# Dense feed-forward of a two-layer network: gate and up products on moments of a row instead of on the whole row

## The reference, cut to what matters

```python
# layer 0, dense feed-forward; h is the layer-normed x, 2048 rows (4 batches x 512) of 512
gate_w, up_w = spline_reconstruct(gate_cp, 2048, 512), spline_reconstruct(up_cp, 2048, 512)
down_w = spline_reconstruct(down_cp, 512, 2048)
inter = silu(einsum('bsh,ih->bsi', h, gate_w)) * einsum('bsh,ih->bsi', h, up_w)
x = x + einsum('bsi,hi->bsh', inter, down_w)
# layer 1, the scan that the same stage computes beside it (16 states n, 512 channels d, 512 steps, 4 batches)
state = state * exp(dt * A) + (dt * u) * b
y = sum over n of state * c
```

## Time and profile before

| | |
|---|---|
| runs | 1562.31, 1568.68, 1570.82 us |
| profiled execution, first to last instruction | 1567.3 us |
| busy: PE, DVE, ACT, POOL | 1435.0, 1153.4, 918.4, 1062.3 us |
| block B | 180 to 818 us |

### The profile page before, as it was taken

The page is one execution under the profiler, slowest core; times in us unless marked ns, Lnnn a source line. Parts: engine busy times, 40 slices in busy tenths (PEclk is TensorE's granted clock), DMA queues, the critical chain, the costliest instruction groups (busy, mean ns, idle before and its releaser), DMA issues. The chain is left out here.

```text
span 1567.3 us, 26498 instructions
## 1 busy us (share of the span) xinstructions
PE 1435.0 (92%) x6453; PEld 1073.9 (69%) x6454; DVE 1153.4 (74%) x2069; ACT 918.4 (59%) x1420; POOL 1062.3 (68%) x654
## 2 busy tenths in 40 slices
PE   6999878999999999999975559989999999999997
PEld 3444556666666666666644238878988888898886
DVE  5888897888888878888878786656666666565554
ACT  6777677666667666766646664444544444444442
POOL 2222287999999989999941235757666676666675
PEclk9999989999999999999988759999999999999999
DMA  8232557888899889988869416889998899888876
GB/s 314 96 111 98 180 132 144 179 197 205 192 196 217 186 195 178 221 188 195 176 150 336 159 31 159 193 193 209 198 200 192 191 206 201 203 186 190 189 146 118
DMA packets 106416, 283.95 MB, mean 181 GB/s; under 512 B 16641, under 2 KB 18850, under 8 KB 95090
## 3 DMA queue, kind: packets, MB, share of 16 engines
q0 software_dynamic: 43520, 155.57, 50.0%
q1 hardware_dynamic: 60322, 123.12, 26.4%
q10 hardware_dynamic: 2512, 4.52, 0.8%
HBM read 152.28 MB, written 135.08 MB: 183 GB/s over the span
## 5 line engine op out<-in xcount | busy, mean ns | idle before, releaser
L1156 POOL TENSOR_TENSOR B_E<-B_dtu,B_BC 128x512 f32<-128x512 f32 (+3 forms) x121 | 309.3, 2670 | 16.7 <-DMA B_BC<-bc_d 16.7
L2080 POOL DMA_INDIRECT out_x<-D_y,D_rows x144 | 243.8, 1693 | 75.4 <-issue 43.6
L889 ACT ACTIVATE bank<-B_dtv,negA 128x512 f32<-128x512 f32 x256 | 173.5, 690 | 159.8 <-DVE B_E L1024 98.1
L1024 DVE TENSOR_TENSOR_SCAN B_E<-bank,B_E 128x512 f32<-128x512 f32 x192 | 230.2, 1214 | 42.5 <-ACT bank L889 34.8
L1162 POOL TENSOR_TENSOR B_E<-B_E,B_BC 128x1536 f32<-128x1536 f32 x64 | 234.0, 3656 | 34.5 <-DVE B_E L1024 29.8
L2045 POOL DMA_INDIRECT D_rows<-rows_d,D_source x144 | 155.9, 1083 | 129.0 <-DMA out_x<-D_y,D_rows 62.3
L806 PE MATMUL bank<-B_Wd,B_inter 128*128 128x512 f32 x512 | 231.9, 606 | 9.0 <-DVE X L1011 5.3
L1906 ACT ACTIVATE D_xT_hi<-bank 128x512 fp32r<-128x512 f32 x147 | 88.1, 599 | 231.5 <-PE bank L1815 167.8
L1826 PE MATMUL bank<-W_gu_hi,D_xT_hi 128*128 x584 | 202.4, 347 | 14.5 <-ACT D_xT_hi L1906 13.9
L1968 DVE TENSOR_TENSOR D_xT_lo<-bank,D_xT_hi 128x512 fp32r<-128x512 f32 x147 | 101.3, 689 | 141.1 <-ACT D_xT_hi L1906 108.7
L1827 PE MATMUL bank<-W_gu_lo,D_xT_hi 128*128 x584 | 199.2, 341 | 0.0
(11 more groups left out here) (327 smaller groups left out, 3263.7 us busy)
## 6 DMA issues: line engine op xcount, KB each, us to landing
y_d<-B_E POOLq DMA_DIRECT2D x64, 1024.0 KB, 10.7
B_BC<-bc_d SPq DMA_DIRECT2D x128, 256.0 KB, 6.2
W_raw_gu<-in_wgu SPq DMA_DIRECT2D x64, 384.0 KB
W_raw_d<-in_wd SPq DMA_DIRECT2D x64, 256.0 KB
X<-in_x SPq DMA_DIRECT2D x4, 1024.0 KB, 9.2
y_d<-A_du SPq DMA_DIRECT2D x4, 1024.0 KB, 4.0
dt_d<-A_dtv SPq DMA_DIRECT2D x4, 1024.0 KB, 3.9
dtu_d<-A_dtu SPq DMA_DIRECT2D x4, 1024.0 KB, 4.1
```

Source lines behind the costliest of these rows:

```text
L889: act.activation(dA[m % 2][:, :], dtv[:, c, :], ACT.Exp, scale=negA[:, c, n:n + 1]).then_inc(dA_done, 1)
L1024: v.tensor_tensor_scan(state, dA[m % 2][:, :], E[:, s % NR, c, :], 0.0, ALU.mult, ALU.add).then_inc(s_done, 1)
L1156: g.tensor_tensor(E[:, s % NR, c:end, :], dtu[:, at:at + end - c, :], spread(BC[op % NBC][:, :], end - c), ALU.mult).then_inc(dbu_done, 1)
L2080: g.indirect_dma_start(a["out"], bass.IndirectOffsetOnAxis(ap=rows[i][:, ROW - 1:ROW].bitcast(U32), axis=0), ysb[:, i, :], None, compute_o ...
```

## The change

- The features. For each of eight groups of 256 inner rows (`NG`), rows are sorted so that those of a group have the change of knot at about the same place. For every turn PE first makes F: four matmuls of 32 columns each, side by side in the array by `tile_position`, one for each chunk of 128 hidden values, in plain fp32. 32 features stand for a chunk: four moments each of two runs, and up to 24 values taken plainly. F is split into high and low parts (ACT L936, DVE L1040), and gate and up are products of 128 features: 12 matmuls a turn (L840 to L842) where there were 48.
- The order of turns. All weights are kept on chip (`V_hi`, `V_lo`, `Wd`). The outer loop is over batches, the inner one over the eight groups. Turned X is made for one batch at a time, in the last turn of the batch before.
- The down product sums four chunks in PSUM before it is added to X: `sums_at(jj)` gives two tiles a turn of 4 matmuls each. The number of matmuls is the same, the additions are two a turn instead of four, and both go through one bank (`Y_bank`, bank 5) because bank 4 holds F. The products of a turn are used one to three turns later (`NI` is 8), and the last four tiles come behind the last turn.
- 24 weight units, not 48: one for gate and up of a group and sixteen for down. All lie in turns 0 to 6, one to five a turn. Masks and powers are loaded three units ahead by ACT (L907, L908), 64 KB each.
- ACT makes both silus of a turn one behind the other, so it changes the table twice a turn instead of four times; F's high part stands behind them, ahead of the decays of the second step.
- Block A: the spline coefficients are plain fp32, without three low parts a batch on DVE (L519).

```diff
-                for ps, W, done in ((first_bank(n), Wg[w], a_ps), (second_bank(n), Wu[w], b_ps)):
-                    for k in range(KC):
-                        hi, lo = (t[:, k, ch * P:(ch + 1) * P] for t in W)
-                        h_hi, h_lo = (t[:, k, tb * L:(tb + 1) * L] for t in (hT_hi, hT_lo))
-                        pe.matmul(ps[:, :], hi, h_hi, start=k == 0, stop=False)
-                        pe.matmul(ps[:, :], hi, h_lo, start=False, stop=False)
-                        mm = pe.matmul(ps[:, :], lo, h_hi, start=False, stop=k == KC - 1)
+            def features(jj):
...
+                for c in range(KC):
+                    mm = pe.matmul(F_bank[c * NF:(c + 1) * NF, :], summed[:, g, c, :], hT[:, c, :], start=True, stop=True, tile_position=(0, c * NF))
+                mm.then_inc(f_ps, 1)
...
+                for ps, col, done in ((first_bank(n), ch * P, a_ps), (second_bank(n), GW + ch * P, b_ps)):
+                    hi, lo = (V[:, g, col:col + P] for V in (V_hi, V_lo))
+                    pe.matmul(ps[:, :], hi, F_hi[:, :], start=True, stop=False)
+                    pe.matmul(ps[:, :], hi, F_lo[:, :], start=False, stop=False)
+                    pe.matmul(ps[:, :], lo, F_hi[:, :], start=False, stop=True).then_inc(done, 1)
+            def down(n, ps):
+                quarter, t = n // 4, n % 4
...
+                elif n:
+                    pe.wait_ge(add_done, n)
...
+                for i in range(4):
+                    mm = pe.matmul(ps[:, :], chunk(4 * quarter + i)[:, t * P:(t + 1) * P], Wd[:, (4 * quarter + i) % NCH, :], start=i == 0, stop=i == 3)
+                mm.then_inc(y_ps, 1)
...
+            for jj in range(TURNS):
                 gate_up(jj, 0)
                 gate_up(jj, 1)
+                sums = sums_at(jj)
+                if jj % NG == NG - 1 and jj < TURNS - 1:
...
+                else:
+                    if jj < TURNS - 1:
+                        features(jj + 1)
+                    for m in turn_units(jj):
+                        weights(m)
+                    for n in sums:
+                        down(n, Y_bank)
+            for t in range(LT):
+                down(2 * TURNS - 4 + t, T_bank[t % 2])
...
+            for jj in range(TURNS):
                 decay(2 * jj, 2)
                 decay(2 * jj, 3)
                 silu(jj, 0)
+                silu(jj, 1)
...
+                if turns:
+                    for t in range(2):
+                        turned(LT * (tb + 1) + t)
+                        normal(LT * (tb + 1) + t + 2)
+                elif jj < TURNS - 1:
+                    feature_hi(jj + 1)
+                for c in range(KC):
+                    if turns and c >= 2:
+                        turned(LT * (tb + 1) + c)
                     decay(2 * jj + 1, c)
+                    for m in after[c]:
+                        unit_first(m)
```

More of the change, by code:

```diff
@@ L104, in spline_constants @@
-    by_down = second.reshape(P, D, NG, 2).transpose(2, 0, 3, 1).reshape(NG, P, 2 * D)
-    masks = np.concatenate([by_gate, by_down], 2)
-    return (table.reshape(P, INTER).astype(np.float32), taps, select.reshape(P, NSEL), powers.reshape(NSEL, KC, 2, P), masks)
+                select[c, ab, :, p, ab, c, p] = 1.0
+    power = np.stack([(np.arange(P) - P // 2.0)**p for p in range(4)]).astype(np.float32)
+    summed = np.zeros((P, NG, KC, NF), np.float32)
+    powers = np.zeros((NG + NCH, 2, NSEL, 2, P), np.float32)
@@ new lines, in spline_constants @@
+    for k in range(NCH):
+        own = order[k * P:(k + 1) * P]
+        at, seg = own % P, own // P
+        to = powers[NG + k].reshape(NCH, 4, 2, P)
+        for m in range(P):
+            to[seg[m], :, 0, m] = power[:, at[m]]
+        masks[NG + k] = second.reshape(P, D, NCH)[at[:, None], np.arange(D)[None], seg[:, None]]
+    units = [u if kind == "gate_up" else NG + u for kind, u in UNITS]
+    table = table.reshape(P, INTER).astype(np.float32)
+    table = np.stack([table[:, order], table.reshape(P, D, NB).transpose(0, 2, 1).reshape(P, INTER)], 1)
@@ L109, in build @@
+    table = table.reshape(P, 2, NB, L).transpose(2, 0, 1, 3)
+    return (table, taps, order, select.reshape(P, NSEL), summed, powers[units].reshape(len(UNITS), 2 * NSEL, 2, P),
+            masks[units].view(np.int32))
 def build(nc, a):
@@ L650, in first_bank, with unit_job, unit_of, chunk_job @@
+        job_of = {job: n for n, job in enumerate(jobs)}
+        def unit_job(m):
+            return job_of[("unit", m, 0)]
+        def unit_of(kind, n):
+            return UNITS.index((kind, n))
+        def chunk_job(jj, ch):
+            return job_of[("gate_up", jj, ch)]
+        def turn_units(jj):
+            before = 1 + sum(len(units) for units in TURN_UNITS[:jj])
+            return list(range(before, before + len(TURN_UNITS[jj]))) if jj < len(TURN_UNITS) else []
         def first_bank(n):
-            return (A_ + dA[:1])[pair(n)]
+            return A_[n % 2]
@@ new lines, in _ @@
+                if jj == 2:
+                    ln_scale()
+                mult(jj, 0)
+                mult(jj, 1)
+                turns = jj % NG == NG - 1 and jj < TURNS - 1
+                units = turn_units(jj)
+                sums = sums_at(jj)
+                if jj < TURNS - 1 and not turns:
+                    feature_lo(jj + 1)
+                if units:
+                    blend(units[0])
+                scan(2 * jj + 1, 0)
+                if units:
+                    unit_lo(units[0])
@@ new lines, in _ @@
+                scan(2 * jj + 1, 1)
+                if sums and not units and not turns:
+                    add(sums[0], Y_bank)
+                for m in units[1:2]:
+                    blend(m)
+                scan(2 * jj + 1, 2)
+                for m in units[2:3]:
+                    blend(m)
+                scan(2 * jj + 1, 3)
+                for m in units[3:]:
+                    blend(m)
+                weigh_last(2 * jj + 1)
+                if sums and (turns or units):
+                    add(sums[0], Y_bank)
```

688 lines of the change are left out of this document (308 added, 380 removed).

## The result

The changed kernel takes 1608.83 us (median of four, 1603.47 to 1620.06) against 1568.95 of the kernel before on the same chip: a ratio of 1.027, with a 95% interval of 1.0219 to 1.032. It is slower; the forecast was 1538 us. The profiled execution spans 1601.7 us, 34.4 more than before.

What follows compares the result with a forecast made beforehand. PE looked like the bound before the change, POOL after it. From the profiled 1567.3 us, + 4 (first turns) - 33 (turns 8 to 31) - 1.5 (block's end) - 0.5 (block A) gave 1536, median 1538; range 1516 to 1568.

Steps and rivals of the forecast that it cites:

- Turns 0 to 6: First turns of block B, holding all units: with turn 7 156.5 us, bounds 141 to 165, some 4 us later than before.
- the chain: Block B, each turn: addition, PE products, ACT and DVE scans in sequence, 14.6 to 16.3 us against POOL's 17.5.
- twelve short operations: Turn 1 of block B: short operations of statistics on DVE instead of additions; the turn was taken as 19 us.
- Loads of masks: First turns of block B: loads issued three units ahead land after 6.4 to 7.1 us; 4 us added over four turns.
- POOL as the bound of turns 8 to 31: Block B: 47 periods of 8.75 us, 414 us with ends of batches, against 447.1 before; gain 33.
- The DMA engines are the wall: Rival, block B: DMA engines asked for 1.00, POOL's pace stays near 9.4 us a step; 1563 to 1570 us; chance 0.10.
- Features: Four feature matmuls a turn on PE in block B: 1.5 us, between 0.8 side by side and 3.2 in a row.
- PE goes cold and the chain passes 19 us: Rival, block B: PE waits each turn and half runs at 1.2 GHz, 20.5 us a turn; 1610 us; chance 0.08.
- the 49 us: Block B before the change: excess of 600 us over POOL's own 551, read as listed waits and waits inside DMA issues.
- The end of the block: End of block B, last product and additions: 1.5 us less than before, between 2 more and 4 less.
- block A: Block A: three DVE operations of about 0.68 us a batch go; gain 0.5 us (0 to 4).
- The signs that I had named: Block B: periods 8.6 to 8.9 us, DVE waits only in turns 0 to 4 and batch ends, one weighing at 350 to 361.

Runs made afterwards that it cites:

- e3: The changed kernel with sums ahead of the units on PE and additions behind later scans on DVE: 1590.34 us, ratio 1.0162.
- e2: The changed kernel with unit matmuls over 128 rows of the array in place of 32 and 64: 1596.41 us, ratio 1.0208.
- e12: Changed kernel with sums first, short statistics on POOL, five buffers, down units spread, joining DMA in four, 32 and 64 rows: 1570.14 us, ratio 1.0017.
- e8: Changed kernel with sums first, 128-row units, short statistics on POOL, five buffers, down units spread over turns 0 to 6: 1564.35 us, ratio 0.9988.
- e11: Changed kernel with sums first, short statistics on POOL, five buffers, units still over 32 and 64 rows: 1564.42 us, ratio 0.9986.
- e1: The changed kernel with the statistics on DVE moved from turns 1 and 2 to turns 9 and 10: 1605.16 us, ratio 1.025.
- e5: The changed kernel with the long statistics on DVE in turn 9 and the two short operations on POOL: 1596.03 us, ratio 1.0218.
- e6: The changed kernel with five buffers for masks and powers in place of four: 1602.18 us, ratio 1.0226.
- e9: The changed kernel with the DMA joining the halves of y made over 4 of its 128 rows: 1593.98 us (one run).
- e4: The changed kernel with the down units' matmuls over 64 columns in place of 512: 1622.40 us, ratio 1.0361.

## Why the prediction was wrong, by its own steps

*The step that failed is "Turns 0 to 6"* (with turn 7): 156.5 us, bounds 141 to 165; measured 209.8. It counted the work of each engine and named the chain, but gave that chain 1 to 3 us a turn. What it should have held, each by an experiment of its own (the sizes overlap, above all the first two):

- The order on two engines, 21.0 us (e3). Scans stood behind additions, additions behind sums, sums behind units, so that units reached POOL. The 21.0 us hold what the clock gave back in turns 2 and 3. The rows of before could not show it, but the order of the changed program did, and I had described this queue for ordinary turns and not for those with units.
- The price of a unit. I took four passes at 0.404 us, 1.6. Warm they took 1.9, and at 1.2 GHz 3.5 to 3.8. Making the clock stay up was worth 16.7 us in the changed kernel (e2), 8.0 between e12 and e8, and 1.2 in e11. I had weighed the low clock for turns 8 to 31 only.
- The statistics, costed as "twelve short operations": 7.8 us (e1) or 16.0 (e5). Two of the twelve wait for POOL, and hold 7.3 us of VectorE (3.07 and 4.27) where others of 128x8 take 0.2. The rows that would have warned me were in the trace of before, on DVE and on POOL: the same operation on 128x8 values ends at 215.53, the weighing at 215.51.

```profile
213.71 1.82 DVE L1060 SCALAR_TENSOR_TENSOR B_dtu<-B_dtu 128x8 f32<-128x8 f32 x1
```

```profile
212.02 3.49 POOL L1162 TENSOR_TENSOR B_E<-B_E,B_BC 128x1536 f32<-128x1536 f32 x1 [4.47 <-DVE B_E L1024]
```

- Loads of masks, 4 us: measured 7.0 (e6). The median from issue to landing was 4.7 us in these turns, below the 6.4 to 7.1 that I took; single loads issued three units ahead came up to 6.7 us late all the same. A median was the wrong figure for it.

*POOL as the bound of turns 8 to 31* was right: 48.06 of 50 us busy, undisturbed periods of 8.6 to 8.7. The size was off by 12.5 us of 414: 7.3 are the joining DMAs (e9); the rest lies in periods of 9.7 to 10.6 us in other steps and was not taken apart. My 8.75 lay between one period in which no join fell (8.61) and an average that holds the joins (8.88); the average would have been nearer. So the rival "The DMA engines are the wall" was there with a part of its size.

*Features*: eight passes took 1.07 us (the row at 254.27), at the cheap end of 0.8 to 3.2 us; I took 1.5.

*The rival "PE goes cold and the chain passes 19 us"* named 1610, and 1608.83 came. It was the right number for the wrong place, by luck. It put the loss in turns 8 to 31; there PE's clock was 0.86 in 600 to 650 and POOL waited 0.9 us for DVE in 380. What was true of it is that a low clock on PE costs when PE's work stands ahead of something that POOL needs; that was so in turns 0 to 4.

*A reading of the rows.* I put what the listed waits left of the 49 us down to waits inside POOL's DMA issues. The list began at 300 us: ahead of it POOL waits 18.0 us more for DVE, from 198 to 300. And the row of an issue overlaps the weighing behind it (518.58 and 0.85 us long, where the next begins at 519.16), so that its length is no sign of a wait. The forecast doesn't hang on this.

*The end of the block* was 0.5 us longer, not 1.5 shorter; block A gave nothing (198.94, to be set beside 198.66).

*The signs that I had named*: the weighing that was at 351.47 came at 396.63 in place of 350 to 361, and waits for DVE stood in all turns up to 7, which both point at the first turns; in turns 9 to 30 the weighings waited for DVE once, 0.9 us; and the last addition ended at 855.14, 16.4 us behind the end of the last weighing.

## What to carry to other kernels

When work is gathered into the start of a loop, write down for those turns alone what each in-order engine has standing behind it, down to the engine that sets the pace; a sum of busy times is no bound there. Then take the causes one by one and together, since causes of 7 to 21 us hid each other here: removing one (e1, e4) showed up partly as a wait for the next, and the gains of two (e2, e3) were largely the same. And where a wait hangs on when a load lands, run the same program more than once before you price it. And a short operation is only short if nothing that it needs is held by another engine.
